# A decoder layer on one core: the causal mask of the query scores from sixteen 32-row products instead of four 128-row products

## The reference

```python
qh = qp.reshape(b, sq, NH, HD).transpose(0, 2, 1, 3)
kh = k.reshape(b, sk, NH, HD).transpose(0, 2, 1, 3)
scores = jnp.einsum('bhqd,bhkd->bhqk', qh, kh) * inv_sqrt_d
causal = jnp.tril(jnp.ones((sq, sk), dtype=bool))
scores = jnp.where(causal, scores, jnp.finfo(scores.dtype).min)
attn = jax.nn.softmax(scores, axis=-1)
out = jnp.einsum('bhqk,bhkd->bhqd', attn, vh)
```

## Time and profile before

| | |
|---|---|
| device time, three runs | 638.14, 643.10, 643.48 us; median 643.1 us |
| span of the profiled execution, first to last instruction | 636.7 us |
| time around the span | at least 1.4 us (against the fastest run), 6.4 us against the median |
| busy: PE, DVE, ACT, POOL | 599.7, 409.6, 278.9, 342.8 us |
| granted TensorE clock, mean | 0.993 of full |

### The profile page before, as it was taken

One profiled execution on the slowest core, in us unless ns is written; L12 is line 12 of the kernel. 1 busy time (PEld: TensorE's weight loads), 2 busy tenths in 40 slices (PEclk: granted clock), 3 DMA queues, 4 the chain that ended last, 5 costly groups with the idle time before them and its releaser, 6 DMA issues.

```text
span 636.7 us, 15520 instructions
## 1 busy us (share of the span) xinstructions
PE 599.7 (94%) x6307; PEld 483.6 (76%) x6307; DVE 409.6 (64%) x841; ACT 278.9 (44%) x637; POOL 342.8 (54%) x462
## 2 busy tenths in 40 slices
PE   7987967979999999999999999999999999999997
PEld 6544545636988889755888889864898888899997
DVE  5997897778744755869644755869762655752221
ACT  4867224232335556342435555251435555343332
POOL 7684145247446667614456666615364666519766
PEclk9999999979999999999999999999999999999999
DMA  8931000020121121011021111002011112014320
GB/s 189 343 104 35 1 1 4 0 68 6 39 67 39 43 60 43 14 34 51 30 80 36 39 52 49 23 17 69 18 51 34 39 44 60 29 38 123 97 55 16
DMA packets 41824, 34.08 MB, mean 54 GB/s; under 512 B 9901, under 2 KB 41206, under 8 KB 41754
## 3 DMA queue, kind: packets, MB, share of 16 engines
q1 hardware_dynamic: 39850, 31.27, 18.2%
q10 hardware_dynamic: 1904, 1.84, 0.9%
HBM read 30.92 MB, written 2.17 MB: 52 GB/s over the span
## 4 chain that ended last, share of the span: by engine, by line
PE 37%; DVE 25%; POOL 13%; issue 9%; ACT 9%; SPq 1%; DMA 1%; POOLq 0%; ACTq 0%; DVEq 0%
DVE A L1574 7%; DVE nm L1652 5%; PE bank L1040 5%; POOL hb L625 3%; PE bank L1237 3%; POOL A L714 3%; PE bank L1044 3%; PE bank L1045 3%; PE bank L1046 3%; PE bank L1084 3%; POOL hT L614 2%; PE bank L1164 2%; POOL hT_last L723 2%; PE bank L1086 2%; PE bank L1085 2%
## 5 line engine op out<-in xcount | busy, mean ns | idle before, releaser
L614 POOL TENSOR_TENSOR hT<-hb,hT 128x256 fp32r<-128x256 f32 (+1 forms) x102 | 78.0, 765 | 72.0 <-ACT hT L789 72.0
L625 POOL TENSOR_TENSOR hb<-hb,cwb 128x256 f32<-128x256 f32 (+1 forms) x102 | 77.0, 755 | 68.6 <-DVE hb L1549 68.5
L1549 DVE TENSOR_TENSOR hb<-hb,bank 128x256 f32<-128x256 f32 (+1 forms) x102 | 42.7, 418 | 101.6 <-ACT hb L799 101.6
L789 ACT ACTIVATE hT<-hb 128x256 fp32r<-128x256 f32 (+1 forms) x102 | 42.4, 416 | 126.0 <-POOL hb L625 125.8
L1044 PE MATMUL bank<-xTf,wGh 128*128 128x256 f32 x272 | 82.9, 305 | 0.0
L1574 DVE TENSOR_TENSOR A<-bank,decay 128x512 f32<-128x512 f32 x128 | 77.4, 682 | 6.0 <-PE bank L1153 5.9
L1045 PE MATMUL bank<-xTf,wGh 128*128 128x256 f32 x272 | 76.7, 282 | 0.0
L1046 PE MATMUL bank<-xTf,wGl 128*128 128x256 f32 x272 | 76.5, 281 | 0.0
L1045 PE MATMUL bank<-xTf,wUh 128*128 128x256 f32 x256 | 72.2, 282 | 0.0
L1046 PE MATMUL bank<-xTf,wUl 128*128 128x256 f32 x256 | 72.1, 282 | 0.0
L1044 PE MATMUL bank<-xTf,wUh 128*128 128x256 f32 x256 | 72.1, 282 | 0.0
(11 more groups left out here) (230 smaller groups left out, 1418.3 us busy)
## 6 DMA issues: line engine op xcount, KB each, us to landing
cwb<-cw_rows SPq DMA_DIRECT2D x54, 128.0 KB, 2.9
A<-cw_rows SPq DMA_DIRECT2D x18, 128.0 KB, 4.0
A<-in_x SPq DMA_DIRECT2D x4, 512.0 KB, 4.3
res<-in_x SPq DMA_DIRECT2D x4, 512.0 KB, 4.8
out_x<-res SPq DMA_DIRECT2D x8, 256.0 KB, 2.4
rawG<-in_L_ffn_w_gate SPq DMA_DIRECT2D x2, 704.0 KB, 6.6
rawU<-in_L_ffn_w_up SPq DMA_DIRECT2D x2, 704.0 KB, 6.6
cwb<-cw_rows SPq DMA_DIRECT2D x12, 112.0 KB, 2.6
```

What stands on the lines that cost most here:

```text
L614: pool.tensor_tensor(hT[hr, c % 2, 1, :], hb[hr, c % 2, :], hT[hr, c % 2, 0, :].bitcast(F32), ALU.subtract).then_inc(h_lo, 1)
L625: pool.tensor_tensor(hb[hr, c % 2, :], hb[hr, c % 2, :], cwb[hr, c % CWS, :], ALU.mult).then_inc(h_scaled, 1)
L789: act.activation(hT[hidden(n), c % 2, 0, :], hb[hidden(n), c % 2, :], ACT.Copy).then_inc(h_hi, 1)
L1549: tt(h, h, up_part(PS[5 + c % 2], n), ALU.mult).then_inc(gu_used, 1)
```

## The change

The constant `maskS` (128x128, upper triangle at -1e30) goes. In its place stands `ahead`, 128 x 224 bf16: in each block of 32 rows, row r holds -1e30 in columns below r + 96 and 0 from there on. One slice of 32 rows and 128 columns, as the stationary operand, with a 32x32 block of the identity repeated four times as the moving one, puts the mask of 32 keys (for four heads) into a bank. So a bank's mask takes four products (j = 0 to 3), and four banks sixteen, where bank i uses row tile i. The order is j outside, i inside, so four products in a row go to four row tiles and four banks. All waits of a sequence now stand before the sixteen; for sequence 0 they wait for the first `q_ready`, and the second is waited for after them.

```diff
-        maskS = sb("maskS", [P, P], BF16)
+        ahead = sb("ahead", [P, P + 96], BF16)
...
-        CONSTS = HEADVAR_MADE + 1 + 3 * GB + 2 + 2 + E + 9 + 3
+        CONSTS = HEADVAR_MADE + 1 + 3 * GB + 2 + 5 + E + 9 + 3
...
-            made(pool.memset(maskS[:], 0.0))
-            made(pool.affine_select(out=maskS[:], in_=maskS[:], compare_op=ALU.is_ge, fill=NEG, base=0,
-                                    pattern=[[-1, P]], channel_multiplier=1))
...
+            made(pool.memset(ahead[:], 0.0))
+            for i in range(4):
+                rows = ahead[32 * i:32 * i + 32]
+                made(pool.affine_select(out=rows, in_=rows, compare_op=ALU.is_ge, fill=NEG, base=-96,
+                                        pattern=[[1, P + 96]], channel_multiplier=-1))
             made(pool.memset(selc[:], 0.0))
...
                             pe.wait_ge(q_ready, g * 2 + 2)
                         elif g and b:
                             pe.wait_ge(p_exp, g * 16 + 4 * (b - 1) + i + 1)
-                        mm(PS[score_base(g, b) + i][:, :], identb[:], maskS[:].unsqueeze(1).to_broadcast([P, 4, P]), start=True, stop=False,
-                           skip_group_check=True)
-                        if b == 0 and i == 2:
-                            pe.wait_ge(q_ready, g * 2 + 2)
+                    if b == 0:
+                        pe.wait_ge(q_ready, g * 2 + 1)
+                    for j in range(4):
+                        for i in range(4):
+                            rows, keys = slice(32 * i, 32 * i + 32), slice(32 * j, 32 * j + 32)
+                            mm(PS[score_base(g, b) + i].rearrange("p (h t) -> p h t", h=4)[:, :, keys], ahead[rows, 96 - 32 * j:96 - 32 * j + P],
+                               identb[rows, 32 * i:32 * i + 32].unsqueeze(1).to_broadcast([32, 4, 32]), start=j == 0, stop=False,
+                               skip_group_check=True)
+                    if b == 0:
+                        pe.wait_ge(q_ready, g * 2 + 2)
```

## The result

| | before | after |
|---|---|---|
| device time, median, same chip | 641.21 us | 647.36 us |
| lowest and highest | 638.14 to 643.48 | 645.47 to 647.83 |
| profiled execution: time, span | 638.14, 636.7 us | 647.23, 645.5 us |
| granted clock, mean of the span | 0.993 | 0.974 |

The ratio is 1.0086, with an interval of 1.0056 to 1.0116. The change makes the kernel 0.9% slower. The forecast was 643.9 us, and the range of 637.0 to 648.5 held the result.

A forecast was written before the change was run, and what follows sets the result against it. It took two nearly equal loops, TensorE's own and one through the other engines, to bound cross attention in groups 1 to 3, and VectorE the start. Masks -1.1 plus constants +1.9 on 643.1 gave 643.9 us, range 637.0 to 648.5.

The forecast's parts named there:

- The mask products: At all sixteen mask places, sixteen small products take 0.23 us instead of 0.97, freeing TensorE of 0.74 us each time.
- Rival (c): At the mask places, strided outputs or issue keep the sixteen products from overlapping; 644.4 us, chance 0.06.
- Sequence 0 of groups 1 to 3: Scores there start 0.32 us earlier behind the second q_ready, gaining 0.96 us over three places.
- Sequences 1 to 3: In groups 1 and 2 these six places give nothing; TensorE's wait for GpSimd's L614 grows instead.
- The 0.1 for group 3: Gain of 0.1 us, bounded 0 to 0.5, in group 3, where TensorE waits only once, 0.2 us.
- Rival (a): TensorE's time is the path, so mask places give most of 0.74 us each; 636.1 or 633.2 us, chance 0.17.
- TensorE's waits in groups 1 and 2: Sign of being right: waits for L614 grow from 0.8 to some 3 us a group, maxima still 16.3 us apart.
- The constants: At the start, building `ahead` delays GpSimd's cut into VectorE's two-operand instructions; first weighing 1.9 us later, bounds +0.5 to +3.3.
- Rival (d): The start is covered, the cut slipping between VectorE's instructions; 642.2 us, chance 0.15.
- Group 0: Its four mask places gain nothing, as the maxima wait for VectorE, not for the scores.
- rival (b): Clock lapses at the start, in TensorE's longer wait for the first weighing; 646.5 us, 649.1 with two lapses, chance 0.12.
- The sum: Mask -1.1 us plus constants +1.9 us makes +0.8 us on the whole kernel, 643.9 us.

The follow-up runs named there:

- e6_b0: Kernel before with `ahead` built at the end of group 0 and the sixteen tiles only at sequence 0 of groups 1 to 3; 639.01 us, ratio 0.9973.
- e7_b123: Kernel before with `ahead` built at the end of group 0 and the tiles only at sequences 1 to 3 of groups 1 to 3; 640.04 us, ratio 0.9984.
- e4_late: Kernel before with `ahead` built at the end of group 0 and the tiles at all twelve places of groups 1 to 3; 639.20 us, ratio 0.9976.
- e2_const: Kernel before plus the five instructions building `ahead` at their new place, read by nobody; 642.04 us, ratio 1.0012.
- e5_idle: Changed kernel with fourteen idle products of 512 columns in TensorE's wait for the first weighing; 642.81 us, ratio to before 1.0039.
- e1_early: Changed kernel with `ahead` built where `maskS` was, ahead of rstd; 643.75 us, ratio to before 1.0040.
- e11_g0: Kernel before with the tiles in group 0 alone and `ahead` built ahead of rstd; 644.34 us, ratio 1.0051.
- e8_fill: e1_early with three idle products of 512 columns ahead of each sequence's sixteen tiles in group 0; 640.45 us, ratio to before 0.9986.

## Why the prediction came out as it did

The time was within the range and within 1%, 3.5 us above the forecast. Part of that is luck: the forecast stood on the 643.1 us of three runs, and six runs of before have their median at 641.2. Forecast was a change of +0.8 us, and measured was +5.5 by the ratio. Point by point:

- **The mask products** (0.97 to 0.23 us): 0.22. Rival (c) is out.
- **Sequence 0 of groups 1 to 3** (-0.96 us): right. The scores start 0.32 us earlier against the second copy. Three places give 1.35 us, somewhat more than forecast; where the other 0.1 us of each comes from is open.
- **Sequences 1 to 3** (absorbed by TensorE's wait): right, shown by e6_b0 against e7_b123, and by e4_late, which with twelve places is no faster than e6_b0 with three. The 0.1 for group 3 wasn't there. Rival (a), TensorE's time as the path, is out: the maxima are 16.29 us apart as before, and a busy share of 94% did not make its time the path.
- **TensorE's waits in groups 1 and 2** (from 0.8 to some 3 us a group, for L614): 2.7 us, of which 1.9 for L614 and 0.8 for the maxima. Right in sum. In group 3, where 0.2 us was the wait before, it is 1.9.
- **The constants** (+1.9 us, bounds +0.5 to +3.3): the mechanism was right, and e2_const and e5_idle show the single meeting of the forecast, at 1.6 us. Rival (d), a start that is covered, is out. In the profiled after it was 4.5 (5.0 less the 0.5 of 12.45), over the upper bound: the bounds left out that a VectorE that is late meets the next GpSimd instructions, too. At equal clock, after against e1_early, it is 2.2, by the ratios 2.9. The Trainium skill's rule ("SBUF — State Buffer", section "Who interferes with whom") holds in both directions: the block that took 1.17 us in after, while VectorE waited, started at 33.09 in e2_const (L580 there) and took 2.74 us, while VectorE's low_bonus went on at 0.34 each.
- **Group 0: "Nothing."** This is the step that failed: the price of the tiles in group 0 was put at nothing. I asked there only whether the scores are waited for, and they aren't. But TensorE waits in that stretch anyway, and with 0.74 us less work at each of four places its clock lapses more often and longer. That cost 3.3 us (e11_g0 against before) and 3.5 us (e1_early against e8_fill, which differ by idle products alone), both by the ratios. The forecast's rival (b) had the price right (2.6 us at most for a lapse; measured 1.9 at the start and some 2.2 between the groups of before's runs) and the place too narrow, the start alone. Its sign did show (a clock of 0.66 from 33 to 48 us), but a lapse there is not the change's own: e4_late, e6_b0 and e7_b123 have it with the start of before. "It decides once the idle stretch comes near the 3.3 us of group 1" was wrong too: a kernel with waits of 1.09 and 0.76 us lapsed there.
- **The sum.** At equal clock after stands 0.6 us above before, against a forecast of +0.8: 2.2 for the constants, -1.35 for the tiles, a rest within the error of a number extrapolated from five runs. The clock's share is (0.987 - 0.972) x 360 = 5.4 us, and I had given it a chance of 0.12, for the start alone. So the sum of what was reckoned came out nearly right, and the greater part of the loss was not in it.

The spread of the three runs shown (638.14 to 643.48) was itself the warning. The profiled before was the lowest of them at a clock of 0.993, so its clean PEclk row said nothing of what the median run does.

Left open: why the clock falls in one execution and not in the next of the same kernel; why the kernels without tiles at sequence 0 differ among themselves by 0.7 us in groups 1 to 3; and whether in group 0 it is the time that TensorE spends in products that counts, or their form, since the idle products of e8_fill are also 128 rows deep, as the old masks were and the tiles are not. No run separates the last two.

## What to carry to other kernels

Before work is taken from an engine whose clock follows its activity, ask what its place looks like afterwards: where the engine waits for others anyway, the saved time only thins its work, and here four masks made shorter in such a stretch cost more (3.3 us) than the twelve others gave (1.5). Where the runs of a kernel differ, set time against granted clock for all of them before anything is compared, since one profiled execution is a draw from several. And build a new constant where GpSimd doesn't read SBUF beside VectorE instructions with two operands there: the same five instructions cost nothing, 0.3, or 0.7 to 3 us, by their place alone.

## What the runs showed of the hardware

- Sixteen bf16 products of 32 rows and 128 columns in four row tiles start 14 ns apart, also where each writes four separate runs of 32 columns.
- The mean granted clock of the same program (before, 101 runs) falls into three groups (0.980 to 0.984, 0.985 to 0.990, 0.991 to 0.995), each a third of the runs, 2.2 us apart.
- Idle products in waits make a kernel faster: 3.5 us in group 0 of the kernel with tiles, for 12 products of 0.23 us each. The Trainium skill, page "TensorE: Matmul & The Clock Gate", section "A second HAM failure mode: psum-queue depth-cycling", tells that short, frequent pauses between groups of products can make the clock go back and forth. The rows of after agree in kind: in group 0's cross attention the clock fell to 0.50 twice, and no wait of TensorE there is above 2.1 us.
- Which of two engines pays for a meeting on SBUF operands can change between executions that come to it alike within 0.01 us, and with it whether the next meeting comes at all. Block and low_bonus met in e5_idle and in after: in one the block took 2.74 us and the twelve low_bonus 3.23, in the other 1.17 and 6.11.
